# Shorter Sinkhorn rounds, and the weights' transposes dealt out in single units

## The reference

```python
x = x + attn_block(layernorm(x))      # gated delta net, 8 heads, then an MLP of 1024
x = x + moe(layernorm(x))
def moe(x):                            # 4096 tokens, 8 experts, F = 1024
    logits = xf @ gate_W.T             # 4096 x 8
    la = -logits / 0.05
    for _ in range(20):
        la = la - logsumexp(la, axis=-1)   # over the 8 experts of a token
        la = la - logsumexp(la, axis=-2)   # over all 4096 tokens of an expert
    pi = exp(la)
    top = top_k(pi, 2)
    g, u = xf @ W_gate[e].T, xf @ W_up[e].T
    y = (silu(g) * u) @ W_down[e].T
    out = y[top0] * pi[:, 0] + y[top1] * pi[:, 1]
```

## Time and profile before

| | us |
|---|---|
| median of 3 runs | 2467.45 (2465.43 to 2468.83) |
| profiled execution | 2468.94 |
| its span | 2467.2 |
| PE busy | 2310.8 (94%) |
| DVE busy | 1811.7 (73%) |
| ACT busy | 1087.4 (44%) |
| mean granted TensorE clock | 0.956 |

### The profile page before, as it was taken

One profiled execution on the slowest core, in us unless ns is written; L12 is line 12 of the kernel. 1 busy time (PEld: TensorE's weight loads), 2 busy tenths in 40 slices (PEclk: granted clock), 3 DMA queues, 4 the chain that ended last, 5 costly groups with the idle time before them and its releaser, 6 DMA issues.

```text
span 2467.2 us, 50463 instructions
## 1 busy us (share of the span) xinstructions
PE 2310.8 (94%) x15131; PEld 2073.5 (84%) x15131; DVE 1811.7 (73%) x4353; ACT 1087.4 (44%) x2287; POOL 759.9 (31%) x1562
## 2 busy tenths in 40 slices
PE   4689999999999999999999999877699999999998
PEld 4578889898889889888898898766599999999887
DVE  6577887887878878878888877377667676667553
ACT  2333344444443443433444443355555455555442
POOL 0113332332332333333323323100234334434332
PEclk9689999999999999999999999855799999999999
DMA  5322212212212122122122121599544545444330
GB/s 189 101 35 46 44 35 48 40 36 50 39 36 53 35 46 45 35 46 42 35 48 41 35 51 27 170 301 307 188 160 147 175 151 175 164 157 164 131 128 18
DMA packets 369741, 232.91 MB, mean 94 GB/s; under 512 B 261612, under 2 KB 343920, under 8 KB 360464
## 3 DMA queue, kind: packets, MB, share of 16 engines
q1 hardware_dynamic: 317136, 200.35, 28.0%
q0 software_dynamic: 11280, 29.31, 4.1%
q10 hardware_dynamic: 41264, 2.51, 1.1%
HBM read 176.19 MB, written 57.67 MB: 95 GB/s over the span
## 4 chain that ended last, share of the span: by engine, by line
PE 87%; DVE 6%; ACT 2%; issue 2%; DMA 2%; SPq 1%; POOL 0%; ACTq 0%; DVEq 0%; POOLq 0%
PE ps_front L778 14%; PE ps_back L2035 11%; PE ps_inva L778 9%; PE ps_invb L778 9%; PE ps_back L778 8%; PE ps_back L2096 5%; PE ps_front L1981 5%; PE ps_back L2079 5%; PE ps_back L2104 5%; PE ps_inva L2001 2%; PE ps_invb L2018 2%; PE ps_front L1974 2%; PE ps_inva L414 2%; PE ps_invb L2020 1%; PE ps_inva L2003 1%
## 5 line engine op out<-in xcount | busy, mean ns | idle before, releaser
L642 DVE TENSOR_TENSOR w_lo<-w_raw,w_hi 128x512 fp32r<-128x512 f32 x288 | 190.1, 688 | 4.0 <-ACT w_hi L730 0.2
L778 PE MATMUL ps_back<-w_hi,eh_hi 128*128 128x256 f32 x624 | 180.1, 289 | 3.2 <-DVE eh_lo L652 3.2
L778 PE MATMUL ps_back<-w_lo,eh_hi 128*128 128x256 f32 x624 | 176.4, 283 | 0.0
L778 PE MATMUL ps_back<-w_hi,eh_lo 128*128 128x256 f32 x624 | 176.4, 283 | 0.0
L730 ACT ACTIVATE w_hi<-w_raw 128x512 fp32r<-128x512 f32 x288 | 169.5, 626 | 0.0
L742 ACT ACTIVATE sact<-ps_inva 128x512 f32<-128x512 f32 (+1 forms) x96 | 49.8, 519 | 237.0 <-PE ps_inva L778 198.8
L1364 ACT ACTIVATE v_s<-ps_front 128x512 f32<-128x512 f32 x64 | 38.1, 595 | 248.6 <-PE ps_front L778 248.6
L1364 ACT ACTIVATE g_s<-ps_front 128x512 f32<-128x512 f32 x64 | 38.3, 598 | 238.4 <-PE ps_front L778 229.5
L1269 POOL TENSOR_SCALAR xrow_v<-bag 128x1 f32<-128x1 f32 x31 | 6.8, 220 | 429.0 <-DVE bag L1818 429.0
L778 PE MATMUL ps_inva<-xT_hi,w_hi 128*128 128x512 f32 (+1 forms) x384 | 135.3, 352 | 1.9 <-DVE xT_lo L647 1.7
L1981 PE MATMUL ps_front<-kqT_t 128*128 128x256 f32 x512 | 127.2, 392 | 10.3 <-ACT kqT_t L1388 7.7
(11 more groups left out here) (391 smaller groups left out, 6887.9 us busy)
## 6 DMA issues: line engine op xcount, KB each, us to landing
w_raw<-wts_d SPq DMA_DIRECT2D x72, 1024.0 KB
wts_d<-prep SPq DMA_DIRECT2D x96, 256.0 KB, 3.7
dT<-alphaT_d SPq DMA_DIRECT2D x32, 512.0 KB, 3.7
prep<-L_ffn_W_gate_dram SPq DMA_DIRECT2D x32, 256.0 KB, 3.2
prep<-L_ffn_W_up_dram SPq DMA_DIRECT2D x32, 256.0 KB, 3.6
prep<-L_ffn_W_down_dram SPq DMA_DIRECT2D x32, 256.0 KB, 4.3
x_all<-L_attn_x_dram SPq DMA_DIRECT2D x4, 1024.0 KB, 10.0
hTr<-hT_d SPq DMA_DIRECT2D x32, 128.0 KB, 3.6
```

Of the source, the lines that this page charges most:

```text
L642: V.tensor_tensor(piece(w_lo[p], m).bitcast(F32R), piece(w_raw, m), piece(w_hi[p], m), ALU.subtract).then_inc(split[n], 1)
L778: ins = MM(out_, w[a].bitcast(F32R), x[b].bitcast(F32R), start=start and n == 0, stop=stop and n == 2)
```

## The change

The weights' units are numbered 0 to 95 and dealt out singly (`pe_units`, `act_units`): 24 in the drain (UD), 48 in the rounds (US: two or three a round), 12 in the routing (UR), and the last 12 one or two behind each list build. In the rounds, the first two of a round stand before the column sum's matmul and logarithm ("ahead"), a third behind them ("behind"). In the drain, units 0 and 1 go behind the last level of the last tile's inverse, 2 behind the products with u, 3 to 5 before `state_out`, 6 to 8 behind it, 9 to 14 before `tail_o`, 15 to 17 before `tail_m`, 18 to 20 between `tail_fc` and `tail_proj`, 21 to 23 behind that; ScalarE copies 3 to 8 before tile 30's `tail_x`. SP's order stays.

The first round keeps its maxima. Every later round takes exp(la) once, sums rows, takes the reciprocal of the sums, multiplies (row shares, at most 1), sums columns of the shares, and subtracts both logarithms from `la`. Column maximum, its transpose and spreading, and the second exponential are gone there.

```diff
-        QD, QS = 7, ROUNDS
+        UD, US, UR = 24, 48, 12
+        rinv = r_s[:, 896:896 + TILES]
+        last_units = lambda b: range(*(UD + US + UR + (3 * QN - UD - US - UR) * n // BATCH for n in (b, b + 1)))
+        units_of = lambda n: range(UD + US * n // ROUNDS, UD + US * (n + 1) // ROUNDS)
+        def pe_units(pe, units):
+            for m in units:
+                pe_prepare(pe, 0, m // 3, [m % 3])
+        def act_units(act, units):
+            for m in units:
+                act_prepare(act, 0, m // 3, [m % 3])
 # dve_late, rounds behind the first
+            for n in range(1, ROUNDS):
+                a = FIRST_A + ROUND_A * (n - 1)
+                dve.wait_ge(sk_act, a + 1)
+                ch.link(V.tensor_reduce(rows_, se, X, ALU.add))
+                ch.link(V.reciprocal(rinv, rows_))
+                ch.link(V.tensor_tensor(sd, se, per_head(rinv, E), ALU.mult))
+                ch.mark(V.tensor_reduce(cols_, by_expert(sd), X, ALU.add))
+                dve.wait_ge(sk_act, a + 2)
+                ch.link(V.tensor_tensor(la[:, :, :], la[:, :, :], per_head(rowl, E), ALU.subtract))
+                dve.wait_ge(sk_act, a + 3)
+                ch.link(V.tensor_tensor(la[:, :, :], la[:, :, :], over_tiles(coll), ALU.subtract))
 # act_late
+            ahead, behind = lambda n: units_of(n)[:2], lambda n: units_of(n)[2:]
+            for n in range(1, ROUNDS):
+                d = FIRST_D + ROUND_D * (n - 1)
+                act.wait_ge(sk_dve, d)
+                A(se, la[:, :, :], ACT.Exp).then_inc(sk_act, 1)
+                act.wait_ge(sk_dve, d + 1)
                 A(rowl, rows_, ACT.Ln).then_inc(sk_act, 1)
+                act_units(act, ahead(n))
+                act.wait_ge(sk_pe, FIRST_P + n)
+                A(coll, psB[0][:, 0:E], ACT.Ln, scale=share(n)).then_inc(sk_act, 1)
+                act_units(act, behind(n))
...
-            for c in range(QD + QS, QN):
-                act_prepare(act, 0, c)
+            act_units(act, range(UD + US, UD + US + UR))
             act.wait_ge(tables_made, 2)
             for b in range(BATCH):
                 act.wait_ge(cols_made, b + 1)
                 for n in range(PAIRS_B):
                     ins = A(col_hot[b % 2][:, n, :], col_hot[b % 2][:, n, :], ACT.Copy, scale=tokens[:, b * PAIRS_B + n:b * PAIRS_B + n + 1])
                 ins.then_inc(cols_ready, 1)
+                act_units(act, last_units(b))
 # pe_late
+            for n in range(1, ROUNDS):
+                pe_units(pe, ahead(n))
+                pe.wait_ge(sk_dve, FIRST_D + ROUND_D * (n - 1) + 4)
                 MM(psB[0][:, 0:E], ones[:, :], cols_, start=True, stop=True).then_inc(sk_pe, 1)
+                pe_units(pe, behind(n))
+            pe_units(pe, range(UD + US, UD + US + 3))
...
                 for n in range(PAIRS_B):
                     ins = MM(psB[1][0:COLS, 0:P], col_hot[b % 2][:, n, :], lane_hot[b % 2][:, n, :], start=b == 0 and n == 0, stop=b == BATCH - 1 and n == PAIRS_B - 1)
                 ins.then_inc(pairs_used, 1)
+                pe_units(pe, last_units(b))
 # ScalarE, the last step, ahead of tail_x(t - 1)
-                    act_prepare(act, 0, 0)
+                    act_units(act, range(3, 9))
                 if tail:
                     tail_x(t - 1)
 # TensorE, behind the last step
-            tail_m(TILES - 1), tail_fc(TILES - 1), tail_proj(TILES - 1)
-            pe_prepare(pe, 0, 5), pe_prepare(pe, 0, 6)
+            tail_m(TILES - 1), tail_fc(TILES - 1)
+            pe_units(pe, range(18, 21))
+            tail_proj(TILES - 1)
+            pe_units(pe, range(21, UD))
```

More of the change, by code:

```diff
@@ L313, in program @@
         pre_ps = psI
-        GROUP = ROUNDS
         V3 = lambda a: a.rearrange("p (t e) -> p t e", e=E)
@@ L509, in dve_late @@
             dve.wait_ge(back_evac[BU_LG % 2], b_evac(TILES, BU_LG))
[L510 to L543, removed]
@@ new lines, in dve_late @@
+            ch = Chain(dve, sk_dve)
+            ch.link(V.tensor_reduce(rowm, la[:, :, :], X, ALU.max))
+            ch.link(V.tensor_tensor(sd, la[:, :, :], per_head(rowm, E), ALU.subtract))
+            ch.mark(V.tensor_reduce(colm, by_expert(sd), X, ALU.max))
+            dve.wait_ge(sk_act, 1)
+            ch.mark(V.tensor_reduce(rows_, se, X, ALU.add))
+            dve.wait_ge(sk_pe, 1)
+            ch.mark(V.tensor_reduce(cmx, psF[0][0:E, 0:P], X, ALU.max))
+            dve.wait_ge(sk_act, 2)
@@ new lines, in dve_late @@
+            ch.link(V.tensor_tensor(sd, sd, per_head(rowl, E), ALU.subtract))
+            dve.wait_ge(sk_pe, 2)
+            ch.link(V.tensor_tensor(la[:, :, :], sd, over_tiles(psF[1][:, 0:E]), ALU.subtract))
+            dve.wait_ge(sk_act, 3)
+            ch.mark(V.tensor_reduce(cols_, by_expert(se), X, ALU.add))
+            dve.wait_ge(sk_act, FIRST_A)
+            ch.link(V.tensor_tensor(la[:, :, :], la[:, :, :], over_tiles(coll), ALU.subtract))
+            assert ch.n == FIRST_D
+            for n in range(1, ROUNDS):
[8 more added lines that the diff above has]
+                dve.wait_ge(sk_act, a + 3)
+                ch.link(V.tensor_tensor(la[:, :, :], la[:, :, :], over_tiles(coll), ALU.subtract))
@@ L697, in act_late @@
             act.preload_act_table_set("natural_log_exp_and_others")
[L698 to L702, removed]
-                A(rowl, rows_, ACT.Ln).then_inc(sk_act, 1)
[L704 to L714, removed]
+            share = lambda n: 1.0 if n == ROUNDS - 1 else E / TOKENS
+            ahead, behind = lambda n: units_of(n)[:2], lambda n: units_of(n)[2:]
+            act.wait_ge(sk_dve, 2)
+            A(se, sd, ACT.Exp).then_inc(sk_act, 1)
+            act.wait_ge(sk_dve, 4)
+            A(rowl, rows_, ACT.Ln).then_inc(sk_act, 1)
+            act.wait_ge(sk_dve, 7)
+            A(se, la[:, :, :], ACT.Exp).then_inc(sk_act, 1)
+            act_units(act, ahead(0))
+            act.wait_ge(sk_pe, FIRST_P)
+            A(coll, psB[0][:, 0:E], ACT.Ln, scale=share(0)).then_inc(sk_act, 1)
+            act_units(act, behind(0))
+            for n in range(1, ROUNDS):
+                d = FIRST_D + ROUND_D * (n - 1)
+                act.wait_ge(sk_dve, d)
+                A(se, la[:, :, :], ACT.Exp).then_inc(sk_act, 1)
+                act.wait_ge(sk_dve, d + 1)
+                A(rowl, rows_, ACT.Ln).then_inc(sk_act, 1)
+                act_units(act, ahead(n))
+                act.wait_ge(sk_pe, FIRST_P + n)
+                A(coll, psB[0][:, 0:E], ACT.Ln, scale=share(n)).then_inc(sk_act, 1)
+                act_units(act, behind(n))
             act.wait_ge(sk_dve, SK_D)
@@ L782, in pe_late @@
             MM = nc.tensor.matmul
[L783 to L790, removed]
+            ahead, behind = lambda n: units_of(n)[:2], lambda n: units_of(n)[2:]
+            pe.wait_ge(sk_dve, 3)
+            nc.tensor.transpose(psF[0][0:E, 0:P], colm, ident[:, :]).then_inc(sk_pe, 1)
+            pe.wait_ge(sk_dve, 5)
+            MM(psF[1][:, 0:E], cmx.to_broadcast([E, P]), ident[0:E, 0:E], start=True, stop=True).then_inc(sk_pe, 1)
+            pe_units(pe, ahead(0))
+            pe.wait_ge(sk_dve, 8)
+            MM(psB[0][:, 0:E], ones[:, :], cols_, start=True, stop=True).then_inc(sk_pe, 1)
+            pe_units(pe, behind(0))
+            for n in range(1, ROUNDS):
+                pe_units(pe, ahead(n))
+                pe.wait_ge(sk_dve, FIRST_D + ROUND_D * (n - 1) + 4)
                 MM(psB[0][:, 0:E], ones[:, :], cols_, start=True, stop=True).then_inc(sk_pe, 1)
[L792 to L796, removed]
+                pe_units(pe, behind(n))
+            pe_units(pe, range(UD + US, UD + US + 3))
             pe.wait_ge(rt_dve, 13)
@@ L799, in pe_late @@
             MM(V3(psF[1][:, 0:TE]), ones[:, :], both, start=True, stop=True).then_inc(rt_pe, 1)
-            for c in range(QD + QS + 2, QN):
-                pe_prepare(pe, 0, c)
+            pe_units(pe, range(UD + US + 3, UD + US + UR))
             for b in range(BATCH):
@@ L1491, in step @@
                 copy_last_t(t)
+                if not more:
+                    act_units(act, range(0, 2))
                 if tail:
@@ L1499, in step @@
                 copy_u(t, more)
+                if not more:
+                    act_units(act, range(2, 3))
                 if more:
@@ L1536, in _ @@
             step(TILES - 1, 1, False, False, True)
-            act_prepare(act, 0, 1), act_prepare(act, 0, 2)
+            act_units(act, range(9, 15))
             tail_o(TILES - 1)
-            act_prepare(act, 0, 3), act_prepare(act, 0, 4)
+            act_units(act, range(15, 18))
             tail_m(TILES - 1), tail_fc(TILES - 1)
-            act_prepare(act, 0, 5), act_prepare(act, 0, 6, [0, 1])
+            act_units(act, range(18, UD))
             tail_x(TILES - 1)
@@ L2145, in step @@
                 level_t(t, p, L0 + 1)
+                if not more:
+                    for g in range(G):
+                        pe.wait_ge(t_ready[g], 2 * t + 2)
```

(19 more changed lines are left out.)

5 lines of the change are left out of this document (2 added, 3 removed).

## The result

The changed kernel takes 2502.36 us (median of 4 runs, 2501.78 to 2506.42) against 2466.44: ratio 1.0145, 95% interval 1.0132 to 1.0158. It is 36 us slower; the forecast was some 27 slower (2494), its range up to 2507. The profiled execution took 2501.78, its span 2500.0, 32.8 more than before.

What follows compares the result with a forecast made beforehand. Matmuls bound the kernel outside the middle; there one instruction chain ends each stage. Drain +10.9, rounds -17.2, routing 0, builds +26, join +6.8 sum to +26.5: 2494 us, range 2478 to 2507.

Steps and rivals of the forecast that it cites:

- the largest term: List builds: TensorE and ScalarE take turns over the added units, at a clock between half and full; +26 us.
- rival 4: Builds: TensorE takes unit transposes once their bank is free, not behind the matmuls; faster, 2459 us; chance 0.07.
- the drain: Last tile's tail: copies waiting for quarter 0's store delay tile 30's logits and all queued behind; +10.9 us (7 to 13).
- the join: Last build to expert matmuls: last units delay the w_raw load and so the experts' start; +6.8 us (4.5 to 8).
- Rival 2: List builds run at half clock throughout, costing +32.6 us, join +0.3; total 2501 us; chance 0.19.
- Rounds: Sinkhorn rounds: chain shortens from 5.06 to 3.85 us a round, 102.3 to 85.1 in all; -17.2 us.
- the third unit: Rounds with three units: its copy delays the next exponential by 0.81 us, in seven rounds.
- DMA isn't the new limit: Rounds: five rounds move four quarters at 5.2 us each, against 5.06 before, so transfers don't bind.
- bound of -22.9: Rounds: the largest gain forecast, in us, if the third unit costs nothing.
- rival 3: Drain: quarter 0's store lands before ScalarE reaches unit 6, so the 11.2 us wait goes; 2483 us; chance 0.08.
- rival 1: List builds run at full clock and cost 19.7 us; total 2488 us; chance 0.18.
- Routing: VectorE chain between rounds and builds: unchanged, 0 us, up to +1.5 if four quarters' transfers run over.

Runs made afterwards that it cites:

- experiment 1: Changed kernel, but on TensorE each list build's unit transposes stand ahead of that build's matmuls, ScalarE's order kept: 2471.35 us, ratio 1.0005.
- experiment 4: Changed kernel, but a round's third copy is made in the next round, behind the row logarithm: 2500.08 us, ratio 1.0119.
- experiment 2: Changed kernel, but ScalarE copies units 6 to 8 behind tile 30's tail_x instead of ahead of it: 2504.13 us, ratio 1.0145.
- Experiment 3: Changed kernel, but with the drain of the kernel before (21 units, old places) and 15 units instead of 12 between rounds and builds: 2494.24 us, ratio 1.0096.
- experiment 9: Changed kernel plus sixteen unused transposes of a constant behind each of the first seven builds' units: 2488.88 us, ratio 1.0086.
- 8: Changed kernel with old drain, third copies a round late, build transposes ahead of matmuls, two units in each of the first six builds: 2453.97 us, ratio 0.9948.
- 10: Changed kernel, drain and rounds kept, with build transposes ahead of matmuls and two units in each of the first six builds: 2462.95 us, ratio 0.9975.
- 7: Changed kernel with old drain, third copies a round late, all twelve last units behind the rounds and none in the builds: 2464.70 us, ratio 0.9988.
- experiment 5: Changed kernel with old drain, 15 units behind the rounds, empty builds, three units a round, third copied a round late: 2462.10 us, ratio 0.9977.

## Why the prediction was right

**Direction and mechanism of the largest term.** The builds go in turns because batch b's unit stands behind batch b's matmuls; rival 4, that TensorE would run ahead, fell in the trace (ScalarE waits 4.29 us for a unit's transposes) and in experiment 1. The total owes something to terms that missed in opposite directions: the drain came out 2.4 us cheaper than forecast, the builds 5.2 and the join 1.9 dearer. Rival 2, with 2501, lies nearer to 2502 than my 2494.

**Rounds: right in sum, 85.5 for 85.1, with a little luck.** The chain (3.85, reciprocal 0.35 for 0.36 assumed) and the third unit (4.61 to 4.64 in all seven rounds, for 4.66) came as worked out. The step that failed is "DMA isn't the new limit". I compared averages (5.2 us a quarter against 5.06); four copies waited 4.8 us for stores all the same. That cost the chain little. One wait fell where a third unit waits anyway; the other three made rounds of two units last 4.48, 4.02 and 4.14, and the eleven two-unit rounds together took 0.9 us more than 11 times 3.85. The first round (6.07 for 6.3) and the cheaper third units (0.77 for 0.81) gave back half of that. My bound of -22.9 for a free third unit was wrong: experiment 4 got 2.5 of 5.7.

**Drain: the place right, the cause only half.** la came at 1588.82 for 1589.2. I counted the wait of units 12 to 14 as 0.3 us on top; it is a second wait, which alone keeps the oT copies just as late, so rival 3 (take the 11.2 out) was mispriced, as experiment 2 shows. The sum came out 2.4 too high: quarter 0's store landed no later than before (1585.86, where I had added 0.5, though this execution was 1.2 late already), and the Wo matmuls ran at full clock, 3.72 against 6.52. Of that 2.8, the fc matmuls gave back 1.6 (5.47 against 3.84 before). Experiment 3 gives the term: 8.5.

**Builds: the mis-sized term, +31.2 for +26.** I took the middle between a full and a half clock, 46 us for seven turns; they took 49.6, and the eighth build's matmuls, which I left at 1.94, 3.41. Six builds' matmuls ran at 3.3 to 3.6 (behind waits of 2.8 to 3.1 us), the first at 3.67 behind a long wait, the second at 2.87. That is rival 2's mechanism for the matmuls, though not for all units: from the third build on these ran at 0.60 to 0.65, near or at full clock. Rival 2's total fits because two of its rows missed in opposite directions. Its 1.09 for a unit was too much, and its 3.05 for the matmuls wasn't half clock throughout: the profile has a granted clock of 0.59 there (1745 to 1748), and the build ahead of it shows what sixteen matmuls cost at 0.50:

```profile
1741.67 3.67 PE L809 MATMUL ps_back<-k_s,y 128*78 128x128 f32 x16 [6.62 <-ACT y L760]
```

For rival 1 the turns' 39.6 and the last batch's 4.2 make 43.8, near what experiment 9 then gave: 44.5. The Trainium skill ("TensorE: Matmul & The Clock Gate", section "What's actually happening") has the default state throttled and activity releasing it; the traces agree, 3.61 behind a 3.11 us wait in the changed kernel and 1.94 behind one of 1.09 in experiment 9.

**Join: +8.7 for +6.8.** The order of steps was as worked out; w_raw's load took 11.7 us from issue (1794.44 to 1806.10) and not 9.6. The row gathers ran beside it; whether they made it slower isn't shown. In experiments 8 and 10 it took 10.6 and 10.4, and the join was down to 13.9 and 13.7.

**Routing: +0.6.** The two products met the half clock (1.22 and 1.06 us, where before had 0.70 and 0.59). Routing took 24.6 to 24.7 in every experiment but 7.

## What to carry to other kernels

Filler work on two in-order engines needs its producer's half placed ahead of the chain's instruction and its consumer's half behind it; both behind makes the two engines take turns, and here the clock fell too. Before putting filler whose buffer waits for a store in front of an evacuation, follow everything that is queued behind it, and look for a second such wait that ends at the same time. Shortening a chain beside saturated transfers gives only what the transfers leave: of the 23 us that I had worked out for the chain alone, 8 came with a quarter a round and 17 to 20 with 0.8.

## What the runs showed of the hardware

A reciprocal on VectorE costs 1753 ns for 128x256 and 0.35 us for 128x32, so by an estimate from these two sizes about 6.3 ns an element of a partition and 0.15 us fixed, where a product of 128x256 takes 0.43. Extra transposes without any use made the builds 10.7 us faster through the granted clock, which rose from 0.72 over the builds to 0.91, the cold first build included (experiment 9). Without them the matmuls of the last six builds, each behind a wait of 2.8 to 3.1 us, ran at 0.51 to 0.54, and the units right behind them at 0.90 to 1.00. Loads and stores in pieces of 256 KB together reached 341 GB/s at share 1.01 (experiment 5).
